# Conv, linear, expert and window attention layers on one core: the two expert stages routed in halves, with half of the window attention moved in between

## The reference

```
x = conv_attention(x)                       # scores over 1024 pixels, gamma * out + x
x = iternorm_whiten(x) * weight + bias
t = to_tokens(x)                            # [8, 1024, 128]
t = t + linear_attention(ln(t))             # 8 heads of 16
t = t + gelu_experts(ln(t))                 # L2_ffn: 8 experts, 512 wide, the best 2 per token
t = t + window_attention(ln(t))             # L3_attn: windows of 32 tokens, shifted by 16, per image
t = t + silu_experts(ln(t))                 # L3_ffn: 8 experts, 341 wide (w1, w3, w2), the best 2
```

## Time and profile before

| | |
|---|---|
| three runs | 1769.05, 1755.12, 1762.91 us |
| their median | 1762.91 us |
| the profiled execution | 1768.02 us, of which the span is 1766.3 us |
| mean granted TensorE clock | 0.839 of full speed |
| TensorE busy | 1309.2 us, 74% of the span |
| VectorE busy | 1027.7 us, 58% |
| POOL busy | 641.1 us, 36% |
| ScalarE busy | 516.6 us, 29% |

### The profile page before, as it was taken

One profiled execution on the slowest core, in us unless ns is written; L12 is line 12 of the kernel. 1 busy time (PEld: TensorE's weight loads), 2 busy tenths in 40 slices (PEclk: granted clock), 3 DMA queues, 4 the chain that ended last, 5 costly groups with the idle time before them and its releaser, 6 DMA issues. The chain is left out here.

```text
span 1766.3 us, 33584 instructions
## 1 busy us (share of the span) xinstructions
PE 1309.2 (74%) x12214; PEld 1120.0 (63%) x12216; DVE 1027.7 (58%) x2452; ACT 516.6 (29%) x1169; POOL 641.1 (36%) x645
## 2 busy tenths in 40 slices
PE   6999985375914888988995772857519999799950
PEld 3555564265914888888984441535519999789950
DVE  3777756998461333345454764645626776577841
ACT  3444420121202444444443331315103232222220
POOL 3000000342316665645353013004046666654554
PEclk9999996687556999999998885865559999899985
DMA  7200000003002333333221000003012323233331
GB/s 284 91 0 1 1 3 4 0 1 108 0 14 77 100 100 107 100 94 101 89 90 40 6 12 25 4 7 91 0 49 87 120 91 120 86 102 95 97 130 56
DMA packets 90551, 114.08 MB, mean 65 GB/s; under 512 B 18982, under 2 KB 74146, under 8 KB 90402
## 3 DMA queue, kind: packets, MB, share of 16 engines
q1 hardware_dynamic: 70818, 66.41, 12.0%
q0 software_dynamic: 19584, 45.65, 7.7%
HBM read 54.84 MB, written 57.15 MB: 63 GB/s over the span
## 5 line engine op out<-in xcount | busy, mean ns | idle before, releaser
L1316 POOL DMA_INDIRECT gx_fetch<-sorted_results,g_places x128 | 126.5, 988 | 223.4 <-DVE tokens L1505 119.3
L1298 POOL DMA_INDIRECT sorted_rows<-s_normed,s_places x128 | 145.2, 1134 | 120.5 <-DMA sorted_rows<-s_normed,s_places 50.9
L1392 PE MATMUL g_bank<-g_w_down,gx_hT 128*128 x1472 | 185.5, 281 | 0.0
L1392 PEld LDWEIGHTS g_bank<-g_w_down,gx_hT 128*128 128x128 f32 x1472 | 178.5, 198 | 0.1
L1298 POOL DMA_INDIRECT sorted_rows<-g_normed,g_places x128 | 130.8, 1022 | 123.4 <-DMA sorted_rows<-g_normed,g_places 53.3
L1316 POOL DMA_INDIRECT sx_fetch<-sorted_results,s_places x128 | 132.3, 1033 | 109.7 <-DMA sx_fetch<-sorted_results,s_places 59.7
L1357 PE MATMUL s_bank<-sx_xT_high,sx_w_now 128*128 128x256 f32 x552 | 164.6, 298 | 1.1 <-issue 0.6
L1358 PE MATMUL s_bank<-sx_xT_low,sx_w_now 128*128 128x256 f32 x552 | 156.2, 283 | 0.0
L1359 PE MATMUL s_bank<-sx_xT_high,sx_w_now 128*128 128x256 f32 x552 | 156.2, 283 | 0.0
L1392 PE MATMUL s_bank<-s_w_down,sx_hT 128*128 x1104 | 142.3, 279 | 9.2 <-issue 7.5
L1357 PE MATMUL g_bank<-gx_xT_high,gx_w_now 128*128 128x256 f32 x368 | 113.6, 309 | 44.9 <-DVE gx_w_now L1445 18.7
(11 more groups left out here) (388 smaller groups left out, 2901.8 us busy)
## 6 DMA issues: line engine op xcount, KB each, us to landing
gx_xq<-sorted_rows SPq DMA_DIRECT2D x92, 128.0 KB
sorted_results<-gx_yq SPq DMA_DIRECT2D x92, 128.0 KB
sx_xq<-sorted_rows SPq DMA_DIRECT2D x92, 128.0 KB
sorted_results<-sx_yq SPq DMA_DIRECT2D x92, 128.0 KB
sorted_rows<-zeros POOLq DMA_DIRECT2D x20, 512.0 KB, 12.9
feats<-in_x SPq DMA_DIRECT2D x8, 512.0 KB, 6.3
out<-s_normed SPq DMA_DIRECT2D x16, 256.0 KB
g_raw_up<-in_L_ffn_W SPq DMA_DIRECT2D x1, 2048.0 KB, 10.8
```

What stands on the lines that cost most here:

```text
L1298: pool.indirect_dma_start(out=self.sorted_rows[g], out_offset=bass.IndirectOffsetOnAxis(ap=places[:, at, r:r + 1], axis=0), in_=self.norme ...
L1316: pool.indirect_dma_start(out=fetch[n % 2][:, i, r, :], out_offset=None, in_=self.sorted_results[g], in_offset=bass.IndirectOffsetOnAxis(a ...
L1392: done = pe.matmul(down[u % 2][:, P * k:P * k + C], hT[u % 2][0:width, i, P * k:P * k + P], self.w_down[0:width, bass.ds(e, 1), i, :].rear ...
```

## The change

The expert stages work on two halves of 32 tiles (four images). Parts that stood behind one another now run beside each other:

- A class `Plan` replaces the global table: the gelu stage has groups [32, 32] with 39 + 39 = 78 units, the silu stage [32, 24, 8] with 39 + 31 + 15 = 85, where both had 92. The scratch in DRAM is four arrays of 39, 39, 31 and 15 units, shared by both stages, and takes 32 DMAs to fill.
- `route` becomes a class `Route` whose methods work on one half. The norm (`PartNorm`) takes statistics of 32 tiles; the normalised rows are written into `normed` directly, by VectorE and ScalarE (in gelu 4 of 8 tiles of an image by VectorE in the first half and none in the second; in silu 4 in both), and POOL copies nothing. The operations of the placing are the same on half the elements.
- In the gelu routing block POOL sends group 0 while TensorE, ScalarE and VectorE route the second half. The window's tables (`WindowTables`, with 32 small copies more on POOL) and the weights' low parts, now on VectorE, stand in this block too.
- The second gelu block has the units, the 64 sends of group 1, the window attention over images 0 to 3, and behind it on VectorE all additions that are left; the additions from step 49 are those of group 0.
- The silu stage has three blocks: weights and the routing of the first half; the window attention over images 4 to 7, beside the 64 sends of group 0, and behind it the routing of the second half; the units with the sends of groups 1 and 2, the fetches and the images' stores. The additions begin at steps 49 (group 0) and 79 (group 1).

Its core:

```diff
-GROUP_TILES = [8, 16, 24, 16]
-GROUPS = len(GROUP_TILES)
-GROUP_UNITS = [(2 * n * P + E * (UNIT - 1)) // UNIT for n in GROUP_TILES]
 class Plan:
...
+        self.units = [(2 * n * P + E * (UNIT - 1)) // UNIT for n in tiles]
...
+GELU_PLAN = Plan([32, 32], [(0, 1), (1, 2)])
+SILU_PLAN = Plan([32, 24, 8], [(0, 1), (1, 3)])
...
         adds = {}
-        for start, tiles in ((52, range(FIRST_TILE[2])), (FIRST_UNIT[3] + self.TO_DOWN + 6, range(*FIRST_TILE[2:4]))):
-            for i, n in enumerate(tiles):
+        for start, g in self.adds:
+            for i, n in enumerate(range(self.plan.first_tile[g], self.plan.first_tile[g + 1])):
...
 def gelu_and_first_half(nc, ins, ident, tokens, tables, sorted_rows, sorted_results):
...
+            @block.gpsimd
+            def _(pool):
+                route.constants_of(pool)
+                tables.gpsimd(pool)
+                pool.wait_ge(route.placed, 1)
+                send_group(pool, plan, 0, normed, places, group_rows, sent)
...
+            @block.vector
+            def _(dve):
+                steps = Steps(dve, route.steps_sem)
+                route.norm.take_stats(dve, tokens, 0)
+                route.norm.finish(dve, steps, 0)
+                for b in range(PB):
+                    route.normalise_by_vector(dve, b)
+                route.norm.take_stats(dve, tokens, 1)
+                for b in range(PB):
+                    route.take_scores(dve, b)
+                route.norm.finish(dve, steps, 1)
+                dve.wait_ge(setup.loaded[3], 32)
+                route.place(dve, steps, 0)
+                for b in range(PB, PB + 2):
+                    route.take_scores(dve, b)
+                setup.vector(dve)
+                for b in range(PB + 2, B):
+                    route.take_scores(dve, b)
+                route.place(dve, steps, 1)
...
+        units = Units(t, kind, plan, sent, w_up, w_down, up_bias, down_bias, ident, tokens, normed, gates, places,
+                      owners, group_rows, group_results, "gx_", banks, ((49, 0),))
+        window = WindowAttention(t, "w1_", tables, tokens, 0, PB, banks, normed[:, :, :])
...
         @block.gpsimd
         def _(pool):
-            units.send(pool)
-            window.make_masks(pool)
+            for g in range(1, plan.groups):
+                send_group(pool, plan, g, normed, places, group_rows, sent)
             units.bring(pool)
...
         @block.vector
         def _(dve):
             units.vector(dve)
             window.vector(dve, units)
+            units.add_until(dve, TT)
...
+def silu_and_second_half(nc, ins, ident, tokens, tables, sorted_rows, sorted_results, out):
...
+            with ExitStack() as second:
+                window = WindowAttention(Tools(nc, second), "w2_", tables, tokens, PB, B, banks, normed[:, PT:TT, :])
+                block = second.enter_context(nc.Block())
...
+                @block.gpsimd
+                def _(pool):
+                    send_group(pool, plan, 0, normed, places, group_rows, sent)
...
+                @block.vector
+                def _(dve):
+                    window.vector(dve)
+                    steps = route.steps
+                    route.norm.take_stats(dve, tokens, 1)
+                    route.norm.finish(dve, steps, 1)
+                    for b in range(PB, B):
+                        route.normalise_by_vector(dve, b)
+                    for b in range(PB, B):
+                        route.take_scores(dve, b)
+                    route.place(dve, steps, 1)
...
+        units = Units(t, kind, plan, sent, w_up, w_down, None, None, ident, tokens, normed, gates, places, owners,
+                      group_rows, group_results, "sx_", banks, ((49, 0), (79, 1)))
```

1095 lines of the change are left out of this document (646 added, 449 removed).

## The result

The changed kernel takes 1794.38 us (median of four runs, 1787.92 to 1802.51) where the kernel before, run beside it, takes 1764.38 (four runs, 1755.12 to 1769.05): 1.018 times as long, 95% interval 1.0135 to 1.0225. The forecast was 1758, its range ended at 1785. The profiled execution has a span of 1786.2 us at a mean granted clock of 0.804. It is the shortest of the four (1787.92 us), and that of the kernel before (1768.02) one of the longer, so the two profiles are 19.9 us apart where the medians are 30.0; the other 10 us stand in neither of them.

What follows compares the result with a forecast made beforehand. No one engine bounds the whole: two long stages are bound by PE, three shorter by small-instruction chains or POOL's indirect DMAs. Terms +23.3 - 56.8 - 37.9 + 103.4 - 36.8 = -4.8 us on 1762.9 give 1758 us, range 1730 to 1785.

Steps and rivals of the forecast that it cites:

- Window over the second half, with the sends beside it: Silu stage, window attention over images 4 to 7: 120 us and 2 for POOL's neighbourhood, 122, ending at 1300.8.
- The 64 sends (some 105 us) are hidden: Second window: POOL's 64 sends of silu group 0 run beside it and add nothing beyond 2 us.
- a second window over 135: Sign in the profile after that the forecast is wrong: the second window taking over 135 us, where 122 was expected.
- slower rival: Second window: POOL's sends hold up VectorE, 30 us longer, 1788; over 1% slower from 22.5 us; chance 0.18.
- rule of the shared ports: VectorE and GpSimd share ports as an exclusive lock; VectorE's casts would often wait a whole 0.95 us instruction.
- Gelu routing: From 418.2 us through routing and first sends to the first gelu unit at 572.5, 23.3 us later than before.
- Gelu units: Gelu stage: 92 units become 78, 77 steps take 321 us, ending at 905.5; 56.8 us saved.
- faster rival: Gelu units run at the silu units' pace, up to 17 us quicker; 1736 with quicker silu routing; chance 0.27.
- first window and fetches: End of the gelu stage: window over the first half 120 us, then 48 fetches 88; 208, ending at 1113.8.
- the second half's routing: Silu stage behind the second window, alone: 46 us, then 3.9 to the first silu unit at 1350.7.
- the silu units and the end: From the first silu unit through the last fetches to the end at 1761.5: 410.8 us, before 447.6.
- silu weights: Start of the silu stage, weights and first half of routing: 62 us plus 3, bounds 50 and 85, ending at 1178.8.

Runs made afterwards that it cites:

- a1: The changed kernel with POOL's 64 silu sends waiting until the second window half is over; 1797.88 us.
- a4: The changed kernel with 64 more indirect DMAs of 64 KB each, which nothing reads, beside the first window; 1843.07 us.
- b0: The kernel before, run again without an edit on chip 6; 1737.96 us.
- b1: The changed kernel with the whole window attention back in the gelu stage and silu routed as gelu is, on chip 6; 1726.55 us in one execution.
- d1: The changed kernel with nothing changed, run a third time, on chip 4; 1785.02 us, ratio 1.0184 to the kernel before.
- a2: The changed kernel with the 64 indirect sends of silu group 0 replaced by plain DMAs of the same bytes, issued by SyncE; 1744.56 us.
- c1: The changed kernel with the 64 indirect sends beside the second window going to consecutive rows, on chip 10; 1734.45 us.
- c2: The changed kernel with POOL waiting after each of the 64 sends in place of every fourth, on chip 10; 1737.76 us.

## Why the prediction was wrong

- **The step that failed** is the term "Window over the second half, with the sends beside it": 122, measured 156.7. "The 64 sends (some 105 us) are hidden" was wrong in the one sense I had not priced: POOL's time was hidden, but TensorE's 32x32 matmuls beside it were held up. On chip 9 the window takes 113.7 alone and 154.4 with the sends, 0.64 us a send or 40.7 in all (a1 and a4); the term had 120 and 2. The prediction had named this sign of being wrong itself: a second window over 135.
- **The slower rival** had the right place and nearly the right size (+30, 1788) by the wrong mechanism. VectorE's eight w_logit subtractions have the same length with and without the sends, and its 154 instructions in the window are busy for 62.96 us without (a1) and 63.10 with them (a4). The Trainium skill's rule of the shared ports (SBUF — State Buffer, "Who interferes with whom") is thus not what makes this loss: VectorE's instructions grew by 0.14 us in all, where 22.5 would have decided. That holds for POOL issuing DMAs; beside POOL's own arithmetic stands.
- **The trace of before had it.** The prediction prices what sends do to VectorE and has no line on TensorE beside a fetch in the window. There, with POOL's fetches from 1011.8 on, stands the same trickle:

```profile
1012.25 0.57 PE L1748 MATMUL g_bank<-g_normed 32*32 32x32 f32 x42
1013.13 0.23 PE L1748 MATMUL g_bank<-g_normed 32*32 32x32 f32 x3 [0.31 <-issue]
1013.86 0.26 PE L1748 MATMUL g_bank<-g_normed 32*32 32x32 f32 x4 [0.50 <-issue]
1014.64 0.23 PE L1748 MATMUL g_bank<-g_normed 32*32 32x32 f32 x2 [0.52 <-issue]
1015.38 0.18 PE L1748 MATMUL g_bank<-g_normed 32*32 32x32 f32 x1 [0.51 <-issue]
1016.11 0.24 PE L1748 MATMUL g_bank<-g_normed 32*32 32x32 f32 x1 [0.55 <-issue]
1017.55 1.09 PE L1748 MATMUL g_bank<-g_normed 32*32 32x32 f32 x61 [1.20 <-issue]
```

  From 1012.82, where the 42 end, to 1017.55, one us after POOL's fourth fetch, 11 matmul instructions start, and 4.7 us pass. At that rate 64 DMAs would cost some 75 us (an estimate, and an upper bound, since many DMAs meet no such matmuls). The rows show the trickle and that it can be dear; they do not give the 34.7.
- **Gelu routing**: 9.5 too low, of which the start of the sends (471.1 for 464.8) is 6.3; the rest is the sends' own pace.
- **Gelu units**: 21.9 too high. 77 steps in 300.3 are 3.90 a step, so the faster rival (up to 17) came true beside the slower one. How much of it the change made shows on chip 6: a step takes 3.90 in b0, the kernel before, and 3.71 in b1, which has the changed gelu stage, so 0.19 a step or 14.6 us for 77. On the first kind a step is longer beside POOL's sends than without them (4.01 and 3.63 in d1); that fewer of them are the whole reason is not shown.
- **Right**: first window and fetches (209.8 for 208.3), the second half's routing (50.9 for 49.9), the silu units and the end (405.4 for 410.8). The silu weights were 5.3 too low.
- **The sum.** The forecast was -4.8 and the span's change +19.9: 24.7 apart, of which +34.7 is the window, +9.5 the gelu routing, -21.9 the gelu units, and +2.4 the other four. Without the 34.7 the span would have come out 14.8 us shorter than before, 10 below the forecast. a2 (which has it not, on a chip of the first kind) took 1744.56 where before took 1755.35, in one execution each. By the medians of the measurement (+30.0) it is 34.8 and not 24.7 apart, and no profile shows where the other 10 lie.

**What stays open.** Why chips 7, 9 and 4 are held back and 6, 15, 10 and 13 hardly (the same programs ran on 7 and 6, and on 4 and 15; chip 13 had only small matmuls); what in an indirect DMA's issue reaches TensorE's issue; and what the changed kernel itself takes on the second kind: only c1 and c2, which differ from it in how they send, ran there, in one execution each.
